# Fp32r transposes for the attention and adjacency tiles of a four-layer graph network, and one tile turned by both forms

## The reference

```
x = layernorm(x + L0(x, adj))   # five small graph convolutions on the first 25 nodes only
x = layernorm(x + L1(x, adj))   # z = x W^T + bW; e = leaky(ai + aj^T), masked where adj <= 0;
                                # att = softmax([e, sink]); att @ z
x = layernorm(x + L2(x, adj))   # relu(((1+eps) x + adj @ x) W1 + b1) W2 + b2
x = layernorm(x + L3(x, adj))   # silu(rmsnorm((eps x + adj @ x) W1 + b1) * w) W2 + b2
```

## Time and profile before

| | |
|---|---|
| median of three runs | 2746.48 us (2746.43 to 2747.16) |
| the profiled execution's own time | 2746.2 us |
| span from its first to its last instruction | 2744.4 us |
| mean granted TensorE clock | 0.988 |
| PE busy | 2644.1 us, 96% |
| DVE busy | 2022.4 us, 74% |
| ACT busy | 1561.2 us, 57% |
| POOL busy | 1277.7 us, 47% |
| one graph in the middle, from one `turn_att(b, 2)` to the next | 161.8 us |

### The profile page before, as it was taken

The page is one execution under the profiler, slowest core; times in us unless marked ns, Lnnn a source line. Parts: engine busy times, 40 slices in busy tenths (PEclk is TensorE's granted clock), DMA queues, the critical chain, the costliest instruction groups (busy, mean ns, idle before and its releaser), DMA issues.

```text
span 2744.4 us, 41122 instructions
## 1 busy us (share of the span) xinstructions
PE 2644.1 (96%) x14650; PEld 2267.5 (83%) x14650; DVE 2022.4 (74%) x4504; ACT 1561.2 (57%) x2911; POOL 1277.7 (47%) x1384
## 2 busy tenths in 40 slices
PE   6499999999999999999999999999999999999997
PEld 5478888888888888888888888888888888888986
DVE  5776877868687786868878686786868778686735
ACT  2437557464755756466565646656475575647524
POOL 2243554535455354545635454553635545354533
PEclk9799999999999999999999999999999999999998
DMA  7030402204040120403113040220404022040200
GB/s 225 18 127 1 154 1 77 77 3 152 1 130 25 59 96 1 154 1 109 46 39 116 1 154 1 89 66 23 132 1 154 1 82 74 8 146 1 78 1 16
DMA packets 205224, 181.00 MB, mean 66 GB/s; under 512 B 17367, under 2 KB 186718, under 8 KB 205022
## 3 DMA queue, kind: packets, MB, share of 16 engines
q1 hardware_dynamic: 197454, 177.04, 20.1%
q10 hardware_dynamic: 7568, 1.34, 0.3%
HBM read 161.15 MB, written 17.19 MB: 65 GB/s over the span
## 4 chain that ended last, share of the span: by engine, by line
PE 89%; ACT 3%; DVE 3%; issue 1%; POOL 0%; ACTq 0%; POOLq 0%; DVEq 0%
PE bank L945 13%; PE bank L949 13%; PE bank L946 12%; PE bank L1024 9%; PE bank L1010 8%; PE bank L995 6%; PE bank L996 6%; PE bank L1000 6%; PE bank L1028 4%; PE bank L910 4%; PE bank L896 4%; PE bank L975 3%; PE bank L1042 1%; ACT att L1205 1%; PE bank L923 1%
## 5 line engine op out<-in xcount | busy, mean ns | idle before, releaser
L945 PE MATMUL bank<-mt_hi,x_hi 128*128 128x512 f32 x1536 | 630.2, 410 | 0.3 <-ACT x_hi L1196 0.3
L949 PE MATMUL bank<-mt_hi,x_lo 128*128 128x512 f32 x1536 | 602.3, 392 | 0.0
L946 PE MATMUL bank<-mt_lo,x_hi 128*128 128x512 f32 x1536 | 600.5, 391 | 0.0
L1370 POOL TENSOR_TENSOR rstd<-ve,neg_half 128x4 f32<-128x4 f32 x126 | 160.9, 1277 | 411.6 <-DVE ve L1546 410.0
L949 PEld LDWEIGHTS bank<-mt_hi,x_lo 128*128 128x128 f32 x1536 | 289.1, 188 | 63.8 <-POOL x_lo L1375 0.2
L945 PEld LDWEIGHTS bank<-mt_hi,x_hi 128*128 128x128 f32 x1536 | 289.9, 189 | 54.3 <-ACT scratch L1241 4.2
L946 PEld LDWEIGHTS bank<-mt_lo,x_hi 128*128 128x128 f32 x1536 | 290.6, 189 | 50.2
L1606 DVE TENSOR_TENSOR sq_sum<-sq_sum,scratch 128x512 f32<-128x512 f32 x224 | 154.7, 691 | 228.8 <-ACT scratch L1241 228.8
L995 PE MATMUL bank<-a_hi,W_lo 128*128 128x512 f32 x768 | 318.3, 414 | 2.9 <-ACT hid L1222 2.9
L996 PE MATMUL bank<-a_hi,W_hi 128*128 128x512 f32 x768 | 301.6, 393 | 0.0
L1169 ACT ACTIVATE mt_hi<-bank 128x512 fp32r<-128x512 f32 x256 | 153.0, 598 | 236.0 <-PE bank L910 236.0
(11 more groups left out here) (168 smaller groups left out, 6092.2 us busy)
## 6 DMA issues: line engine op xcount, KB each, us to landing
att<-in_adj SPq DMA_DIRECT2D x128, 512.0 KB, 7.9
adj_col<-in_adj SPq DMA_DIRECT2D x256, 256.0 KB, 3.0
out<-x_even SPq DMA_DIRECT2D x64, 128.0 KB, 2.8
out<-x_odd SPq DMA_DIRECT2D x64, 128.0 KB, 2.7
x_odd<-in_x SPq DMA_DIRECT2D x56, 128.0 KB, 4.3
x_even<-in_x SPq DMA_DIRECT2D x49, 128.0 KB, 3.8
G<-in_L_gnn_W SPq DMA_DIRECT2D x2, 2048.0 KB, 19.2
W_raw<-in_L_gnn_W SPq DMA_DIRECT2D x2, 1024.0 KB, 9.7
```

What stands on the lines that cost most here:

```text
L945: nc.tensor.matmul(dst[:], hi, mt_hi[:, k, cols], start=k == 0, stop=False)
L946: nc.tensor.matmul(dst[:], hi, mt_lo[:, k, cols], start=False, stop=False)
L949: mm = nc.tensor.matmul(dst[:], lo, mt_hi[:, k, cols], start=False, stop=done)
```

## The change

The transposes of `turn_att` and `turn_col` are issued in fp32r form instead of fp32. For this the attention tile gets a second name `att_r` of type fp32r at the same address, `turn_col` reads the raw block under the name `mt_lo` instead of `adj_col`, the PSUM bank is addressed as fp32r, and an fp32r identity `ident_r` is made once by POOL in the prologue. The transposes of `aj_rows`, `rms_row` and the prologue stay fp32.

Beside that, four tiles of graph 0 are turned a second time, in fp32 form, into `out_bank[0]`, between `turn_att(0, 0)` and `turn_att(0, 1)`. DVE copies that bank to `sq_sum`, subtracts it from the bank that the fp32r form filled, and adds the difference, times 1e9, to `b23_row` in two steps of 256 columns. These four DVE instructions stand ahead of `turn_lo(0, 0)`. POOL's first `add_bias` of layer 3's bias waits for them.

```diff
@@ adj_resnorm
+        with ExitStack() as place:
+            att_r = sb("att_r", [P, NT, NODES], F32R, place)
         att = sb("att", [P, NT, NODES])
+        ident_r = sb("ident_r", [P, P], F32R)
@@ prologue, gpsimd
                                         pattern=[[-1, P]], channel_multiplier=1).then_inc(s_ident, 1)
+                pool.wait_ge(s_ident, 4)
+                nc.gpsimd.tensor_copy(ident_r[:], ident[:])
                 nc.gpsimd.memset(H_all[:], 0.0).then_inc(s_pad, 1)
@@ turn_att
-                        mm = nc.tensor.transpose(turn_bank[i][:, j * P:(j + 1) * P],
-                                                 att[:, 4 * i + j, k * P:(k + 1) * P], ident[:])
+                        mm = nc.tensor.transpose(turn_bank[i][:, j * P:(j + 1) * P].bitcast(F32R),
+                                                 att_r[:, 4 * i + j, k * P:(k + 1) * P], ident_r[:])
@@ turn_col
-                src = adj_col[:, k, half_cols(h)]
+                src = mt_lo[:, k, half_cols(h)]
                 for j in HALF_TILES:
                     cols = slice(j * P, (j + 1) * P)
-                    mm = nc.tensor.transpose(turn_bank[i][:, cols], src[:, cols], ident[:])
+                    mm = nc.tensor.transpose(turn_bank[i][:, cols].bitcast(F32R), src[:, cols], ident_r[:])
@@ tensor, ahead of the first graph
-            for k in range(2):
-                turn_att(0, k)
+            turn_att(0, 0)
+
+            for j in HALF_TILES:
+                mm = nc.tensor.transpose(out_bank[0][:, j * P:(j + 1) * P], att[:, j, 0:P], ident[:])
+            mm.then_inc(s_same, 1)
+            turn_att(0, 1)
@@ gpsimd, add_bias
+                if norm == 2 and b == 0 and t == 0:
+                    pool.wait_ge(s_differ, 3)
@@ vector, after denominators(0)
+            dve.wait_ge(s_same, 1)
+            dve.wait_ge(s_turned[0], turn_att_use(0, 0) + 1)
+            nc.vector.tensor_copy(sq_sum[:], out_bank[0][:]).then_inc(s_same, 1)
+            dve.wait_ge(s_same, 2)
+
+            dve.wait_ge(s_turn_hi[0], 1)
+            nc.vector.tensor_tensor(sq_sum[:], turn_bank[0][:], sq_sum[:], ALU.subtract).then_inc(s_differ, 1)
+            dve.wait_ge(s_differ, 1)
+            nc.vector.scalar_tensor_tensor(out=b23_row[:], in0=sq_sum[:, 0:D], scalar=1.0e9, in1=b23_row[:],
+                                           op0=ALU.mult, op1=ALU.add).then_inc(s_differ, 1)
+            dve.wait_ge(s_differ, 2)
+            nc.vector.scalar_tensor_tensor(out=b23_row[:], in0=sq_sum[:, D:], scalar=1.0e9, in1=b23_row[:],
+                                           op0=ALU.mult, op1=ALU.add).then_inc(s_differ, 1)
+            dve.wait_ge(s_differ, 3)
             for k in range(NT):
                 turn_lo(0, k)
```

More of the change, by code:

```diff
@@ L95, in adj_resnorm @@
         s_l0_stored = sem("layer0_stored")
-        graph0 = (att, x_even, sq_sum, stat0, mv0, ve, rstd, qi, qj, ai, aj)
+        graph0 = (att, att_r, ident_r, x_even, sq_sum, stat0, mv0, ve, rstd, qi, qj, ai, aj)
         graph0_sems = (s_att_in, s_stats0, s_aggr0, s_var0, s_rstd0, s_y0, s_sums, s_ai, s_aj, s_l0_stored)
@@ L115, in prologue @@
              eps2, L2_W1, L2_b1, L2_W2, L2_b2, eps3, L3_W1, L3_b1, rms_w, L3_W2, L3_b2, x_l0):
-    att, x_even, sq_sum, stat0, mv0, ve, rstd, qi, qj, ai, aj = graph0
+    att, att_r, ident_r, x_even, sq_sum, stat0, mv0, ve, rstd, qi, qj, ai, aj = graph0
     s_att_in, s_stats0, s_aggr0, s_var0, s_rstd0, s_y0, s_sums, s_ai, s_aj, s_l0_stored = graph0_sems
@@ L723, in layers @@
     s_cov = sem("bias_scaled")
+    s_same, s_differ = sem("same_tile_turned"), sem("difference_taken")
     s_mask, s_leaky, s_masked, s_top, s_exp = sem("mask"), sem("leaky"), sem("masked"), sem("row_tops"), sem("exps")
```

## The result

The changed kernel takes 2729.22 us (median of 4 runs, 2728.89 to 2733.19) against 2746.45 us in the same session; the ratio is 0.994, with an interval of 0.9927 to 0.9954. It is faster by 17 us, where 59 were forecast. The time lies within the wide range of 2655 to 2757 us, but outside the 2655 to 2720 of the case that I took for the likeliest; it falls among the times of the "paces between", 2720 to 2745, to which I gave 0.03.

The account below looks back on a forecast made before the run. PE, busy 96% of the span, was taken as the bound, with DVE nearly limiting in one stretch. From 2746.2 us, a net saving of 63 (80 - 16 - 1) and 4 for the doubly turned tile gave 2687; range 2655 to 2757.

Parts of the forecast that it names:

- the case that I took for the likeliest: Whole run: fp32r transposes clearly quicker, some 70 ns each on PE, time 2655 to 2720 us; chance 0.60.
- paces between: Remaining case for the transposes on PE: 90 to 105 ns each, time 2720 to 2745 us; chance 0.03.
- What bounds the kernel: PE, busy 96% of the span: a microsecond saved there shortens the run as long as DVE keeps up.
- The pace: Cost of an fp32r transpose on PE: 70 ns instead of 109, saving 80 us over 2048 transposes.
- My sign for a load that rules: Profile after, lines 896 and 910: recorded weight loads would last 0.19 us if the load sets the transposes' speed.
- How much arrives: Share of PE's 80 us that shortens the run: 16 us lost to DVE, 1 in graph 0, net 63.
- the 20%: Between 960 and 1000 us of a graph, half the saving is lost to DVE: 1.0 us per graph, 16 in all.
- The doubly turned tile: Graph 0's start: extra PE and DVE work delays everything after turn_lo(0, 0) by about 3 us; 4 counted, bounds 3 and 8.
- What costs nothing: POOL's identity copy is hidden (0.4 us if uncovered), add_bias's semaphore stands some 100 us earlier, aliases move nothing.
- Nothing gained on PE: Rival: fp32r transposes keep two clocks per column or load at 110 ns; 109 to 112 ns, 2750 to 2757 us; chance 0.20.
- DVE becomes the bound: Rival: transposes quicken but ACT and DVE can't follow, most of 5 us per graph lost; about 2720 us; chance 0.07.
- my formula: Run time for s ns per transpose on PE: 2746.2 - 0.8 x 2.048 x (109 - s) + 5; 2720 at 90, 2666 at 57.

Follow-up runs that it names:

- the probe: form_alone with streams of 24 like transposes added in graph 0, whole or with half the columns; whole: fp32 109 ns apart, fp32r 85 to 86; run 2745.1 us.
- form_alone: The changed kernel without the doubly turned tile, its four DVE instructions and POOL's wait; all 2048 transposes in fp32r form: 2726.99 us.
- double_tile_alone: The kernel before plus the doubly turned tile, DVE's four instructions and POOL's wait, all transposes staying fp32: 2750.63 us.

## Why the prediction failed, point by point

**What bounds the kernel** was right in that the time fell with PE's, but 36 us less of busy PE became 17 us less of time: the condition, that DVE keeps up, failed more often than I allowed for.

**The pace** is the term that was mis-sized. I took 70 ns, from a stream of 67 (53 and 13 on top) that outlasts a load of 60; measured are 85 to 86, and it is the load. That alone would leave 2048 x 24 ns = 49 us of my 80. A whole block gives less, 19 to 20 ns per transpose, as the first matmul behind it begins 86 ns after the last transpose, where it began 28 ns after it before (medians), and with the blocks that save less it is 16.6 ns, 34 us over the run. One half of the argument held: the fp32r stream passes one column per clock, at most 60 ns. The other half, "a load in transpose form takes some 57 to 60 ns", was read off fp32 transposes and carried over to fp32r ones. For fp32 the probe confirms it (62 ns); the fp32r form's load takes 85. I had bounded it from above by the ordinary load's 110 and called the transposing one the nearer row. It lies between. The 13 ns that fp32r matmuls carry at 256 and 512 columns I had put on the stream, with no row that told where they come from; the transposes' stream, at most 60 ns, doesn't have them. My sign for a load that rules was wrong too: I expected recorded loads of 0.19 us, and they last 0.14 with the load ruling.

The sentence on the rule, that transpose mode makes FP32 four times as fast (the Trainium skill, TensorE: Matmul & The Clock Gate, Terms), isn't borne out here: in the probes an fp32 transpose stays at 109 ns, two clocks per column, with a load that needs 62. Against two instructions of about 108 ns, my estimate from rows 5 for an ordinary fp32 matmul of 128 columns, that is twice as fast and not four times.

**How much arrives.** I counted 17 us lost of 80; measured are (11.2 + 3.9) x 16 / 14 = 17 us lost of 34. The sum is the same by chance, since I had expected it for a saving more than twice as large. The step that failed is the 20%: I took half of the saving in the tight stretch as lost and nothing elsewhere, and about half of all was lost. I named the stretch rightly for most of it, and DVE freeing the banks late; I took its length of idle time for the measure of what can be gained. What counted was which instruction stood ahead of the freeing one, and behind that the normalization's chain, which I had not looked at. Nor had I seen the waits of the matmuls behind attention blocks, where I counted nothing lost.

**The doubly turned tile**: DVE's four at 0.69, 0.69, 0.42 and 0.42 us as counted; `turn_lo(0, 0)` begins 2.2 us later instead of 2.8, as the block in front of it had begun 0.5 us sooner. By itself the tile costs 4.1 us, and I had 4. I had counted on a later rise of the clock as part of it. In the profiled executions the granted clock rises from 0.50 to 1.00 at 129.5 us before and at 131.7 in the changed kernel, but at 131.9 in form_alone, which has no tile, and at 133.8 in double_tile_alone. So the changed kernel's later rise can't be put down to the tile, and whether the four extra transposes kept the clock low no run here shows.

**What costs nothing** cost nothing that a run shows; POOL's copy was not tried alone.

**The rivals.** None of the four is it. "Nothing gained on PE" named the right cause, the load, at too high a price. "DVE becomes the bound" was half right, but I had taken it for a matter of 7 in 100. "Paces between" had the time, but for a pace of 90 to 105 ns; the pace of 85 belongs to the likeliest case, and its formula gives 2712 for it.

With the measured pace my formula gives 2746.2 - 0.8 x 2.048 x (109 - 85) + 5 = 2712. Of the 42 us between forecast and result the pace alone makes 25; the other 17 are that a block saves less than the pace says, and that half of what it saves arrives instead of 0.8.

## What to carry to other kernels

The transposes here had two paces, that of their stream and that of their weight load, and the slower one counted. When a change makes one of them faster, measure the other in the new form: a load read off the old form isn't a bound. Two probes with half the columns on one side each settle it in a single run.

When an engine that is busy for 96% of the time becomes faster, look, for each block that moves up, at what the engine behind it does just before it frees the buffer, and at the chain that comes after the last buffer. Idle time added up over a stretch says little. An exchange in an order that removed the visible wait won little here (0.6 us by the medians), since 6.0 of the 8.8 us came back at the next bank and behind it.

## What the runs showed of the hardware

At a granted clock of 1.00 an fp32r transpose of 128 x 128 costs 85 ns in a stream and an fp32 one 109. The fp32r load in transpose form takes 25 ns and 0.47 ns per weight column (32 to 128 columns); the fp32 one takes 48 ns at 96 columns and 62 at 128, which is 21 and 23 less; an ordinary fp32r matmul of 128 columns goes every 111 ns. The number of rows (64 or 128) didn't matter to the fp32r load. The recorded duration of the load, 140 ns in both forms, doesn't show the difference: only the distances between starts do. The first two fp32r transposes of a block are followed after 59 and 65 ns instead of 85. In the probes the load of the first one is recorded 0.23 us ahead of it, under the matmul before; in the stream with 64 rows it isn't, and there the distances are 85 from the first on. At the granted clock of 0.50, in graph 0's first block, fp32r transposes go every 129 ns and fp32 ones every 213.
